# The attention layer's input normalised on GpSimd from pair 8 on, between pieces of GpSimd's preparation work

## The chip, the cores and the metric

The program runs on one core of one Trainium2 chip. The time is the device time of one execution in microseconds. The kernel before took 462.44 us, the median of three runs (461.45 to 463.85).

## The reference

The input x has 32 batches of 256 nodes with 128 features, and there is one 256x256 adjacency matrix. Two layers follow each other, each with a layer norm and a residual:

```
h = max(layernorm(x), 0)
x = x + GAT(h, adj)            # Wh = h W; e = leakyrelu(s1_i + s2_j), masked by adj; softmax(e) Wh
h = max(layernorm(x), 0)
x = x + GCN_LSTM(h, adj)       # twice relu(adj (h Wg + b)), then LSTMs over windows of 1, 2, 3, 4 nodes
```

The layer norm has no weights: (x - mean) / sqrt(var + 1e-5), over the 128 features of a node.

## The kernel before, in words

All of x lies in SBUF in the tensor `xs`, as 64 tiles of 128 nodes by 128 features. Four tiles make a pair of batches, so there are 16 pairs. The attention layer is `phase_a`. Each engine runs its part of it as a software pipeline written out by hand with the helper `ticks`: in tick t an engine works on several stages of different pairs, `live(s)` meaning pair t - s. The engines meet by semaphores alone.

In tick t of `phase_a`, TensorE does in this order: the projection (L926) and the scores' row (L930) of pair t-1, the transposes of the normalised tiles of pair t (L936), the attention's product of pair t-4 (L947) and the transposes of the probabilities of pair t-3 (L959). It waits for `a_v` before the transposes of pair t. VectorE does the two passes over the scores of pair t-1 (L665, L699), with two small operations on 128x4 values between (L673, L677), the reciprocal and the residual of pair t-4 (L706, L713), and the statistics of pair t-5 for the second layer norm (L655). ScalarE copies the projection (L510) and the transposed input (L517, with the ReLU of the layer norm), takes the exponential (L524), normalises pair t (L491, one operation for each of 4 tiles, scale and shift being pointers to one value per partition) and copies the transposed probabilities (L533). `v_norm` holds one pair, so the normalising of pair t waits until pair t-1 is transposed (`a_T`).

GpSimd turns statistics into scale and shift with `norm_scale` (L384 to L393: ten operations on as many columns as there are tiles, one of them a power, L392). For the first layer it does so in groups of 4, 4, 8, 16, 16 and 16 tiles. Then it prepares constants of the second layer in one go: row sums (L407 to L411), the graph weights (L416 to L420), the biases (L422 to L429), the adjacency in the order of the LSTM's windows (L441, L442) and the weights of the first LSTM (L451, L452). Only then comes `norm_scale` for the second layer, for 16 tiles at a time, each time after a wait for the statistics. Then it splits the other LSTM weights. GpSimd issues no DMA. `phase_b`, the graph layer and the first LSTM, follows `phase_a` in the same way and is the first to use all of these constants.

Of the kernel before, what the change touches and what calls it, by code (L numbers as in the profile page):

```python
# [5 lines left out]
def preln_gat_gcn_lstm_kernel(  # L6
# [22 lines left out]
    fp32 = mybir.dt.float32  # L29
    fp32r = mybir.dt.float32r  # L30
    ALU = mybir.AluOpType
# [3 lines left out]
    P = 128  # L35
    assert D == P and N == 2 * P
    TILES = B * N // P
    PAIRS = B // 2
    NODES = B * N
    QUARTER = TILES // 4  # L40
# [10 lines left out]
    GCN_LOADS = 10  # L51
# [7 lines left out]
    with ctx:  # L59
# [7 lines left out]
        xs = sb("xs", [P, TILES, D])  # L67
# [11 lines left out]
        v_norm = sb("v_norm", [P, 4, D])  # L79
# [3 lines left out]
        adjP_hi = sb("adjP_hi", [P, 2, N], fp32r)  # L83
        adjP_lo = sb("adjP_lo", [P, 2, N], fp32r)
        adj_neg = sb("adj_neg", [P, 2, N])
        adjT_hi = sb("adjT_hi", [P, 2, N], fp32r)
        adjT_lo = sb("adjT_lo", [P, 2, N], fp32r)
# [4 lines left out]
        wg_raw = sb("wg_raw", [P, 2, D])  # L92
        wg_hi = sb("wg_hi", [P, 2, D], fp32r)
        wg_lo = sb("wg_lo", [P, 2, D], fp32r)
        b_raw = sb("b_raw", [P, 2, D])
        b_full = sb("b_full", [P, 2, D])
        b_zeros = sb("b_zeros", [P, D])
        b0_parts = sb("b0_parts", [P, D], fp32r)
        b1_parts = sb("b1_parts", [P, 4, D], fp32r)
# [3 lines left out]
        ident = sb("ident", [P, P])  # L103
        ident_r = sb("ident_r", [P, P], fp32r)
# [41 lines left out]
        RUN = [0, 22, 43]  # L146
# [73 lines left out]
        stored = sem("stored")  # L220

        BESIDE = 4

# [131 lines left out]
        @block.gpsimd  # L357
        def _(pool):
            n = 0

            def done(ins):
                nonlocal n
                n += 1
                ins.then_inc(pool_step, 1)
                pool.wait_ge(pool_step, n)

            done(nc.gpsimd.memset(ident[:, :], 0.0))
            nc.gpsimd.affine_select(out=ident[:, :], in_=ident[:, :], compare_op=ALU.not_equal, fill=1.0, base=0,
                                    pattern=[[-1, P]], channel_multiplier=1).then_inc(ident_ok, 1)
            done(nc.gpsimd.memset(b_raw[:, :, :], 0.0))  # L370
            done(nc.gpsimd.memset(b_zeros[:, :], 0.0))
            nc.gpsimd.nop().then_inc(b_zero, 1)
            nc.gpsimd.memset(wh[:, :, :, D + 2:D + 3], 1.0)
            nc.gpsimd.memset(ones[:, :].bitcast(fp32), 1.0).then_inc(ones_ok, 1)
            done(nc.gpsimd.memset(half[:, :], -0.5))


            def norm_scale(which, lo, cnt):
                st = stats[:, which, lo:lo + cnt, :]
                me, qe, mo, qo = st[:, :, 1], st[:, :, 2], st[:, :, 4], st[:, :, 5]  # L380
                a, b, c, d = (v[:, 0:cnt] for v in (ln_a, ln_b, ln_c, ln_d))
                sc, sh = scale[:, which, lo:lo + cnt], shift[:, which, lo:lo + cnt]

                done(nc.gpsimd.tensor_tensor(b, me, mo, ALU.subtract))  # L384
                nc.gpsimd.tensor_tensor(a, qe, qo, ALU.add)
                done(nc.gpsimd.tensor_tensor(d, b, b, ALU.mult))
                nc.gpsimd.tensor_scalar(a, a, 1.0 / D, EPS, ALU.mult, ALU.add)
                done(nc.gpsimd.tensor_scalar(d, d, 0.25, 0.0, ALU.mult, ALU.add))
                nc.gpsimd.tensor_tensor(c, me, mo, ALU.add)
                done(nc.gpsimd.tensor_tensor(a, a, d, ALU.add))  # L390
                nc.gpsimd.tensor_scalar(c, c, -0.5, 0.0, ALU.mult, ALU.add)
                done(nc.gpsimd.tensor_tensor(sc, a, half[:, 0:cnt], ALU.pow))  # L392
                nc.gpsimd.tensor_tensor(sh, c, sc, ALU.mult).then_inc(ln_ok, cnt // 4)  # L393
                pool.wait_ge(ln_ok, which * PAIRS + (lo + cnt) // 4)

            for c, (lo, cnt) in enumerate(X_GROUPS):
                pool.wait_ge(stats_ok, lo + cnt)
                norm_scale(0, lo, cnt)
                if c == FIRST:
                    pool.wait_ge(adjT_in, 16)  # L400
                    done(nc.gpsimd.tensor_copy(adjT_hi[:, :, :], adjT_raw[:, :, :]))
                    nc.gpsimd.tensor_tensor(adjT_lo[:, :, :], adjT_raw[:, :, :], adjT_hi[:, :, :].bitcast(fp32),
                                            ALU.subtract).then_inc(adjT_ok, 1)


            pool.wait_ge(rs_read, 1)
            done(nc.gpsimd.tensor_copy(rs_full[:, :].bitcast(fp32r), rs_raw[:, :]))  # L407
            for b in range(2):
                done(nc.gpsimd.tensor_copy(rs_parts[0:64, b], rs_full[0:64]))
                done(nc.gpsimd.tensor_copy(rs_parts[96:P, b], rs_full[96:P]))  # L410
                done(nc.gpsimd.tensor_tensor(rs_parts[64:96, b], rs_raw[64:96], rs_full[64:96], ALU.subtract))  # L411
            nc.gpsimd.nop().then_inc(rs_ok, 1)


            pool.wait_ge(gcn_w_in, GCN_LOADS * 16)
            done(nc.gpsimd.tensor_copy(wg_hi[:, :, :], wg_raw[:, :, :]))  # L416
            nc.gpsimd.tensor_tensor(wg_lo[:, :, :], wg_raw[:, :, :], wg_hi[:, :, :].bitcast(fp32), ALU.subtract)
            nc.gpsimd.tensor_copy(ident_r[:, :], ident[:, :])
            nc.gpsimd.tensor_tensor(bl[:, :], bl_raw[:, 0], bl_raw[:, 1], ALU.add)
            done(nc.gpsimd.tensor_copy(b_full[:, :, :].bitcast(fp32r), b_raw[:, :, :]))  # L420

            done(nc.gpsimd.tensor_copy(b0_parts[0:32], b_full[0:32, 0]))  # L422
            done(nc.gpsimd.tensor_tensor(b0_parts[32:64], b_raw[32:64, 0], b_full[32:64, 0], ALU.subtract))
            done(nc.gpsimd.tensor_copy(b0_parts[64:P], b_full[64:P, 0]))
            for k in range(4):

                done(nc.gpsimd.tensor_copy(b1_parts[64:P, k], b_zeros[64:P]))
                done(nc.gpsimd.tensor_copy(b1_parts[0:32, k], b_full[0:32, 1]))
                done(nc.gpsimd.tensor_tensor(b1_parts[32:64, k], b_raw[32:64, 1], b_full[32:64, 1], ALU.subtract))  # L429
            nc.gpsimd.nop().then_inc(b_ok, 1)  # L430

            pool.wait_ge(adjT_ok, 1)
            pool.wait_ge(adj_neg_ok, 1)
            for part, placed in ((adjT_hi, adjP_hi), (adjT_lo, adjP_lo)):
                by_t = part[:, :, 0:252].rearrange("p u (a q j) -> p u j q a", q=3, j=4)
                for u in range(2):
                    to = placed[:, u].rearrange("p (j m) -> p j m", j=4)
                    for q in range(3):  # L440
                        nc.gpsimd.tensor_copy(to[:, :, RUN[q]:RUN[q] + 21], by_t[:, u, :, q, :].bitcast(fp32))  # L441
                ins = nc.gpsimd.tensor_copy(placed.rearrange("p u (j m) -> p u j m", j=4)[:, :, :, 21],  # L442
                                            part[:, :, 252:256].bitcast(fp32))
            done(ins)
            nc.gpsimd.nop().then_inc(adjP_ok, 1)

            def split_weights(p, m):
                i, j = (p - 1) // 2, (p - 1) % 2
                for c in range(2):
                    g = slice(c * 2 * D, (c + 1) * 2 * D)  # L450
                    done(nc.gpsimd.tensor_copy(wl_of[0][i][:, j, m, g], wraw[:, m, p - 1, g]))  # L451
                    ins = nc.gpsimd.tensor_tensor(wl_of[1][i][:, j, m, g], wraw[:, m, p - 1, g],  # L452
                                                  wl_of[0][i][:, j, m, g].bitcast(fp32), ALU.subtract)
                ins.then_inc(wl_ok, 1)


            pool.wait_ge(lstm_w_in, 32)
            split_weights(1, 0)
            pool.wait_ge(wl_ok, 1)

            for c in range(4):
                pool.wait_ge(stats_ok, TILES + (c + 1) * QUARTER)
                norm_scale(1, c * QUARTER, QUARTER)


            pool.wait_ge(one_lo, 1)
            for n_, (p, m) in enumerate((p, m) for p in range(2, SKIPS + 1) for m in range(2)):
                split_weights(p, m)
                pool.wait_ge(wl_ok, n_ + 2)

        @block.scalar
        def _(act):
# [23 lines left out]

            def first_norm(t, ph, live):

                if live(0):
                    if isinstance(t, int):  # L500
                        act.wait_ge(ln_ok, t + 1 if t < 7 else PAIRS)
                    after(act, a_T, t, 0)
                    normalise(0, t, range(4), a_v)

# [630 lines left out]
```

## Time and profile before

| | |
|---|---|
| median of three runs | 462.44 us |
| the profiled execution | 464.01 us, span 462.2 us |
| granted TensorE clock, mean of the span | 0.978 |
| PE busy | 433.5 us (94%) |
| VectorE busy | 379.4 us (82%) |
| ScalarE busy | 322.9 us (70%) |
| GpSimd busy | 77.6 us (17%) |

`phase_a` takes about the first 110 us, its full pipeline the stretch from 35 to 95 us. A row of the timeline tells when an instruction or a run of equal ones began, how long it took from its first start to its last end, and in brackets the idle time before it. Starts of the same line in two ticks give the length of a tick.

### The profile page before, as it was taken

To read this page: it belongs to the slowest core of one execution; us is meant where nothing else is said; L and a number is where in the kernel's file an instruction comes from. 1 tells how busy PE (TensorE), PEld (TensorE's weight loads), DVE (VectorE), ACT (ScalarE), POOL (GpSimd) and SP (SyncE) were. 2 spreads that over 40 slices of the span, in tenths; PEclk is the share of its full clock that TensorE was granted. 3 is DMA by queue.
4 is the path that set the end of the run, shared out by engine and by line. 5 is a ranking of instruction groups with operands and counts; after the bars stand their busy time and mean duration, and the time that the engine had idled before them with its cause. 6 is when DMAs were issued, how large, how long until landed. Compare 5 with 4: busy or idle time off the path is not lost.

```text
span 462.2 us, 8017 instructions
## 1 busy us (share of the span) xinstructions
PE 433.5 (94%) x2550; PEld 380.9 (82%) x2550; DVE 379.4 (82%) x976; ACT 322.9 (70%) x632; POOL 77.6 (17%) x182
## 2 busy tenths in 40 slices
PE   6579999979998999999999999999999999999991
PEld 5358888879997999999878888899999988887881
DVE  3799999986779878788777888888788788888895
ACT  3479999966787678887676676767667675564550
POOL 5758841230419100000000000000000000000000
PEclk9689999989999999999999999999999999999998
DMA  8910000000000000000000000000000000002116
GB/s 244 333 41 1 2 2 1 0 0 1 1 3 1 0 0 0 0 0 1 0 0 2 0 2 0 0 1 2 0 1 1 1 1 1 0 23 69 45 48 182
DMA packets 14075, 11.68 MB, mean 25 GB/s; under 512 B 982, under 2 KB 12252, under 8 KB 13788
## 3 DMA queue, kind: packets, MB, share of 16 engines
q1 hardware_dynamic: 11404, 9.97, 7.1%
q10 hardware_dynamic: 2640, 1.33, 1.1%
q8 instruction: 16, 0.26, 0.3%
q14 instruction: 15, 0.12, 0.1%
HBM read 7.10 MB, written 4.19 MB: 24 GB/s over the span
## 4 chain that ended last, share of the span: by engine, by line
PE 69%; DVE 18%; ACT 4%; issue 3%; DMA 3%; DVEq 1%; SPq 1%; ACTq 0%
PE ps L967 47%; PE ps L1089 11%; PE ps L1093 6%; DVE score L699 4%; DVE score L665 3%; DMA xs<-in_x 3%; DVE xs L713 3%; DVE stats L655 2%; PE ps L947 2%; ACT v_norm L491 1%; ACT work L596 1%; DVE xs L848 1%; PE ps L1011 1%; ACT prob L524 1%; PE ps L1007 1%
## 5 line engine op out<-in xcount | busy, mean ns | idle before, releaser
L596 ACT ACTIVATE work<-ps,bl 128x512 f32<-128x512 f32 (+2 forms) x204 | 111.2, 628 | 30.8 <-PE ps L1093 23.4
L967 PE MATMUL ps<-h_hi,wl_hi 128*128 128x512 f32 (+3 forms) x252 | 94.5, 375 | 4.0 <-DVE h_lo L759 3.2
L967 PE MATMUL ps<-h_lo,wl_hi 128*128 128x512 f32 (+3 forms) x252 | 93.9, 372 | 0.0
L967 PE MATMUL ps<-h_hi,wl_lo 128*128 128x512 f32 (+3 forms) x252 | 93.8, 372 | 0.0
L586 ACT ACTIVATE work<-work 128x512 f32<-128x512 f32 (+2 forms) x56 | 31.5, 570 | 44.3 <-DVE work L843 33.6
L967 PEld LDWEIGHTS ps<-h_hi,wl_hi 128*128 128x128 f32 x252 | 47.5, 188 | 11.5 <-issue 3.2
L967 PEld LDWEIGHTS ps<-h_lo,wl_hi 128*128 128x128 f32 x252 | 47.6, 189 | 7.5
L491 ACT ACTIVATE v_norm<-xs,shift,scale 128x128 f32 (+1 forms) x128 | 52.6, 489 | 1.1 <-POOL shift L393 1.0
L967 PEld LDWEIGHTS ps<-h_hi,wl_lo 128*128 128x128 f32 x252 | 47.6, 189 | 6.5
L1089 PE MATMUL ps<-s_hi,wl_hi 128*128 128x512 f32 (+2 forms) x144 | 51.9, 362 | 0.0
L1089 PE MATMUL ps<-s_hi,wl_lo 128*128 128x512 f32 (+2 forms) x144 | 51.4, 359 | 0.0
L569 ACT ACTIVATE s_hi<-ps 128x512 fp32r<-128x512 f32 x48 | 28.4, 601 | 19.9 <-PE ps L967 16.6
L557 ACT ACTIVATE work<-ps,bl 128x512 f32<-128x512 f32 x48 | 30.9, 682 | 9.0 <-DVE work L733 7.6
L947 PE MATMUL ps<-wh,pT 128*128 128x130 f32 x256 | 33.9, 287 | 3.0 <-DVE xs L713 2.5
L947 PEld LDWEIGHTS ps<-wh,pT 128*128 128x128 f32 x256 | 31.1, 196 | 5.7 <-issue 2.9
L1093 PE MATMUL ps<-s_lo,wl_hi 128*128 128x512 f32 (+2 forms) x144 | 34.4, 358 | 0.2 <-DVE s_lo L805 0.2
L794 DVE TENSOR_TENSOR s_hi<-work 128x512 fp32r<-128x512 f32 (+2 forms) x36 | 22.0, 612 | 12.0 <-ACT work L586 11.1
L798 DVE TENSOR_TENSOR work<-work 128x512 f32<-128x512 f32 (+2 forms) x52 | 31.3, 602 | 0.0
L1089 PEld LDWEIGHTS ps<-s_hi,wl_lo 128*128 128x128 f32 x144 | 27.1, 188 | 3.2
L1089 PEld LDWEIGHTS ps<-s_hi,wl_hi 128*128 128x128 f32 x144 | 27.1, 188 | 3.1
L757 DVE TENSOR_TENSOR s_lo<-ps,s_hi 128x512 fp32r<-128x512 f32 x32 | 21.9, 685 | 9.4 <-ACT s_hi L569 9.3
L524 ACT ACTIVATE prob<-score,ebias 128x256 f32<-128x256 f32 x64 | 27.4, 512 | 2.3 <-DVE ebias L677 2.3
(131 smaller groups left out, 968.7 us busy)
## 6 DMA issues: line engine op xcount, KB each, us to landing
result<-xs SPq DMA_DIRECT2D x12, 256.0 KB, 2.3
work<-in_w_ih_t SPq DMA_DIRECT2D x1, 1024.0 KB, 10.0
work<-in_w_hh_t SPq DMA_DIRECT2D x1, 1024.0 KB, 8.7
xs<-in_x SPq DMA_DIRECT2D x2, 256.0 KB, 3.7
xs<-in_x SPq DMA_DIRECT2D x1, 512.0 KB, 7.0
result<-xs SPq DMA_DIRECT2D x4, 128.0 KB, 3.4
result<-xs ACTq DMA_DIRECT2D x4, 128.0 KB, 3.7
adj_raw<-in_adj ACTq DMA_DIRECT2D x1, 256.0 KB, 7.5
```

What stands on the lines that cost most here:

```text
L491: ins = nc.scalar.activation(v_norm[:, k, :], xs[:, bass.ds(i, 1), :].rearrange("p o f -> p (o f)"), ACT.Relu, scale=scale[:, which, bass. ...
L524: ins = nc.scalar.activation(prob[:, m, k], score[:, m, k], ACT.Exp, scale=1.0 - SLOPE, bias=ebias[:, m, k:k + 1])
L557: nc.scalar.activation(one_row(g), ps[:, 4 + g, :], ACT.Tanh if g == G else ACT.Sigmoid, bias=bl[:, g:g + 1]).then_inc(one_act, 1)
L569: nc.scalar.activation(dst, ps[:, s - 1, :], ACT.Copy if s in (1, 3) else ACT.Relu).then_inc(b_hi[s], 1)
L586: nc.scalar.activation(lw[:, par, R_TC, 0:cols], lw[:, par, R_C, 0:cols], ACT.Tanh).then_inc(c_act[par], 1)
L596: nc.scalar.activation(lw[:, par, g, 0:cols], ps[:, 4 * par + g, 0:cols], ACT.Tanh if g == G else ACT.Sigmoid, bias=bl[:, (p - 1) * GATES ...
L794: nc.vector.tensor_tensor(hi, shaped(lw[:, par, O, :]), shaped(lw[:, par, R_TC, :]), ALU.mult).then_inc(c_hi[par], 1)
L798: nc.vector.tensor_tensor(row(r, par, R_H), row(r, par, O), row(r, par, R_TC), ALU.mult).then_inc(c_h[par], 1)
L947: ins = nc.tensor.matmul(psA[:, b, ui * (D + 2):(ui + 1) * (D + 2)], pT[:, 2 * b + uj, ui * P:(ui + 1) * P], wh[:, (ph - 4) % 4, 2 * b + u ...
L967: ins = nc.tensor.matmul(dst, a, b, start=start and n_ == 0, stop=stop and n_ == 2)
L1089: nc.tensor.matmul(ps[:, 4 * par + g, 0:cols], part, s_hi[:, par, 0:cols], start=False, stop=False)
L1093: nc.tensor.matmul(ps[:, 4 * par + g, 0:cols], weights(p, 1, g)[0], s_lo[:, par, 0:cols], start=False, stop=True).then_inc(c_gate[par], 1)
```

## The change

ScalarE normalises only pairs 0 to 7. Pairs 8 to 15 are normalised on GpSimd, by four `tensor_scalar` operations (multiply by scale, add shift) of 128x128 each. They leave out the ReLU, which L517 applies again after the transposes in either kernel. GpSimd's preparation is cut into four pieces, unchanged in their operations, and placed between them. `norm_scale` of the second layer works on 8 tiles at a time: four of its eight calls lie between the pieces, the others behind pair 15.

```diff
-            (the preparation in one go: wg_hi ... b_ok, adjP_ok, split_weights(1, 0))
-            for c in range(4):
-                pool.wait_ge(stats_ok, TILES + (c + 1) * QUARTER)
-                norm_scale(1, c * QUARTER, QUARTER)
+            def first_norm(t):
+                pool.wait_ge(a_T, t)
+                for k in range(4):
+                    i = t * 4 + k
+                    ins = nc.gpsimd.tensor_scalar(v_norm[:, k, :], xs[:, i, :], scale[:, 0, i:i + 1],
+                                                  shift[:, 0, i:i + 1], ALU.mult, ALU.add)
+                ins.then_inc(a_v, 1)
+            def second_scale(h):
+                pool.wait_ge(stats_ok, TILES + 8 * (h + 1))
+                norm_scale(1, 8 * h, 8)
+            first_norm(8)
+            graph_weights()        # L416 to L420
+            second_scale(0)
+            first_norm(9)
+            graph_biases()         # L422 to L429
+            first_norm(10)
+            second_scale(1)
+            first_norm(11)
+            adjacency_order()      # L441, L442
+            first_norm(12)
+            second_scale(2)
+            first_norm(13)
+            step_weights()         # L451, L452 for the first LSTM
+            first_norm(14)
+            second_scale(3)
+            first_norm(15)
+            for h in range(4, 8):
+                second_scale(h)
 (ScalarE)
-                if live(0):
-                    if isinstance(t, int):
-                        act.wait_ge(ln_ok, t + 1 if t < 7 else PAIRS)
+                if live(0) and isinstance(t, int) and t < ON_POOL:      # ON_POOL = 8
+                    act.wait_ge(ln_ok, t + 1)
                     after(act, a_T, t, 0)
                     normalise(0, t, range(4), a_v)
```

## Rows read from the trace of the kernel before

**Rows 1.** Windows; us, then busy time (and instructions) of each engine, TensorE's clock, DMA
```profile
70.00:80.00 10.00, 10.00 (x79) 8.75 (x77) 10.00 (x48) 10.00 (x24) 0.70 (x4) 1.00 0.00 1
```

**Rows 2.** Timeline of VectorE; start us, us, instruction, idle before
```profile
44.60 0.44 DVE L673 SCALAR_TENSOR_TENSOR low<-m,wh 128x4 f32<-128x4 f32 x1
...
60.07 0.15 DVE L673 SCALAR_TENSOR_TENSOR low<-m,wh 128x4 f32<-128x4 f32 x1
...
68.52 0.17 DVE L706 RECIPROCAL rinv<-ps 128x4 f32<-128x4 f32 x1
...
70.01 0.15 DVE L673 SCALAR_TENSOR_TENSOR low<-m,wh 128x4 f32<-128x4 f32 x1
...
94.92 0.17 DVE L673 SCALAR_TENSOR_TENSOR low<-m,wh 128x4 f32<-128x4 f32 x1
```

**Rows 3.** Timeline of ScalarE, one tick
```profile
64.86 0.59 ACT L510 ACTIVATE wh<-ps 128x520 f32<-128x520 f32 x1
...
67.46 1.64 ACT L491 ACTIVATE v_norm<-xs,shift,scale 128x128 f32 x4
69.00 1.01 ACT L533 ACTIVATE pT<-ps 128x1024 f32<-128x1024 f32 x1
69.91 0.59 ACT L510 ACTIVATE wh<-ps 128x520 f32<-128x520 f32 x1
```

**Rows 4.** Timeline of TensorE, the transposes of pairs 7, 9, 10 and 11
```profile
49.47 0.60 PE L936 MATMUL ps<-ident,v_norm 128*128 128x128 f32 x4
...
59.69 0.60 PE L936 MATMUL ps<-ident,v_norm 128*128 128x128 f32 x4
...
64.73 0.60 PE L936 MATMUL ps<-ident,v_norm 128*128 128x128 f32 x4
65.18 2.06 PE L947 MATMUL ps<-wh,pT 128*128 128x130 f32 x16
...
68.84 1.02 PE L930 MATMUL ps<-hT,wa 128*128 128x512 f32 x2
69.70 0.60 PE L936 MATMUL ps<-ident,v_norm 128*128 128x128 f32 x4
```

**Rows 5.** Timeline of GpSimd; starts of the pieces, and one call for 8 tiles
```profile
11.57 0.21 POOL L384 TENSOR_TENSOR ln_b<-stats 128x8 f32<-128x8 f32 x1
...
13.49 1.64 POOL L392 TENSOR_TENSOR scale<-ln_a,half 128x8 f32<-128x8 f32 x1
15.28 0.21 POOL L393 TENSOR_TENSOR shift<-ln_c,scale 128x8 f32<-128x8 f32 x1
...
43.81 0.40 POOL L416 CAST wg_hi<-wg_raw 128x256 fp32r<-128x256 f32 x1 [0.17 <-POOL rs_parts L411]
...
45.84 0.28 POOL L422 CAST b_parts<-b_full 32x128 fp32r<-32x128 f32 x1
...
52.22 1.69 POOL L441 CAST adjP_hi<-adjT_hi 128x84 fp32r<-128x84 f32 x6 [0.23 <-POOL b_parts L429]
...
55.96 0.40 POOL L451 CAST wl_hi<-work 128x256 fp32r<-128x256 f32 x1 [0.17 <-POOL adjP_lo L442]
...
57.58 0.73 POOL L452 TENSOR_TENSOR wl_lo<-work,wl_hi 128x256 fp32r<-128x256 f32 x1
```

**Rows 6.** Groups of GpSimd by shape; busy us, mean ns
```profile
L429 POOL TENSOR_TENSOR b_parts<-b_raw,b_full 32x128 fp32r<-32x128 f32 x4 | 1.8, 460 | 0.3
...
L418 POOL CAST ident_r<-ident 128x128 fp32r<-128x128 f32 x1 | 0.3, 289 | 0.0
```

**Rows 7.** Timeline, a VectorE operation inside a power of GpSimd
```profile
101.90 0.16 DVE L677 SCALAR_TENSOR_TENSOR ebias<-m,low 128x4 f32<-128x4 f32 x1
...
101.82 2.91 POOL L392 TENSOR_TENSOR scale<-ln_a,half 128x16 f32<-128x16 f32 x1
```

**Rows 8.** Timeline of TensorE behind the gap at 98 us, and the graph layer's first product
```profile
100.12 3.31 PE L947 MATMUL ps<-wh,pT 128*128 128x130 f32 x16 [2.11 <-DVE xs L713]
...
104.43 0.36 PE L967 MATMUL ps<-adjT_hi,s_hi 128*128 128x256 f32 x1
```

More of the change, by code:

```diff
@@ L222, in preln_gat_gcn_lstm_kernel @@
         BESIDE = 4
+        ON_POOL = 8
         def ticks(eng, depth, unroll, body, first=0, beside=None, lag=0):
@@ L412, in _ @@
             nc.gpsimd.nop().then_inc(rs_ok, 1)
[L415 to L445, printed above, removed]
             def split_weights(p, m):
@@ L454, in split_weights, with graph_weights @@
                 ins.then_inc(wl_ok, 1)
-            pool.wait_ge(lstm_w_in, 32)
-            split_weights(1, 0)
-            pool.wait_ge(wl_ok, 1)
-            for c in range(4):
-                pool.wait_ge(stats_ok, TILES + (c + 1) * QUARTER)
-                norm_scale(1, c * QUARTER, QUARTER)
+            def graph_weights():
+                pool.wait_ge(gcn_w_in, GCN_LOADS * 16)
+                done(nc.gpsimd.tensor_copy(wg_hi[:, :, :], wg_raw[:, :, :]))
+                nc.gpsimd.tensor_tensor(wg_lo[:, :, :], wg_raw[:, :, :], wg_hi[:, :, :].bitcast(fp32), ALU.subtract)
+                nc.gpsimd.tensor_copy(ident_r[:, :], ident[:, :])
+                nc.gpsimd.tensor_tensor(bl[:, :], bl_raw[:, 0], bl_raw[:, 1], ALU.add)
+                done(nc.gpsimd.tensor_copy(b_full[:, :, :].bitcast(fp32r), b_raw[:, :, :]))
@@ new lines, in graph_biases @@
+            def graph_biases():
+                done(nc.gpsimd.tensor_copy(b0_parts[0:32], b_full[0:32, 0]))
+                done(nc.gpsimd.tensor_tensor(b0_parts[32:64], b_raw[32:64, 0], b_full[32:64, 0], ALU.subtract))
+                done(nc.gpsimd.tensor_copy(b0_parts[64:P], b_full[64:P, 0]))
+                for k in range(4):
+                    done(nc.gpsimd.tensor_copy(b1_parts[64:P, k], b_zeros[64:P]))
+                    done(nc.gpsimd.tensor_copy(b1_parts[0:32, k], b_full[0:32, 1]))
+                    done(nc.gpsimd.tensor_tensor(b1_parts[32:64, k], b_raw[32:64, 1], b_full[32:64, 1], ALU.subtract))
+                nc.gpsimd.nop().then_inc(b_ok, 1)
@@ new lines, in adjacency_order @@
+            def adjacency_order():
+                pool.wait_ge(adjT_ok, 1)
+                pool.wait_ge(adj_neg_ok, 1)
+                for part, placed in ((adjT_hi, adjP_hi), (adjT_lo, adjP_lo)):
+                    by_t = part[:, :, 0:252].rearrange("p u (a q j) -> p u j q a", q=3, j=4)
+                    for u in range(2):
+                        to = placed[:, u].rearrange("p (j m) -> p j m", j=4)
+                        for q in range(3):
+                            nc.gpsimd.tensor_copy(to[:, :, RUN[q]:RUN[q] + 21], by_t[:, u, :, q, :].bitcast(fp32))
+                    ins = nc.gpsimd.tensor_copy(placed.rearrange("p u (j m) -> p u j m", j=4)[:, :, :, 21],
+                                                part[:, :, 252:256].bitcast(fp32))
+                done(ins)
+                nc.gpsimd.nop().then_inc(adjP_ok, 1)
@@ new lines, in step_weights @@
+            def step_weights():
+                pool.wait_ge(lstm_w_in, 32)
+                split_weights(1, 0)
+                pool.wait_ge(wl_ok, 1)
+            def first_norm(t):
+                pool.wait_ge(a_T, t)
+                for k in range(4):
+                    i = t * 4 + k
+                    ins = nc.gpsimd.tensor_scalar(v_norm[:, k, :], xs[:, i, :], scale[:, 0, i:i + 1],
+                                                  shift[:, 0, i:i + 1], ALU.mult, ALU.add)
+                ins.then_inc(a_v, 1)
```

## The prediction

> **What bounds the kernel now.** The change touches only the attention layer, so the first view to read is the busy time by stretches, from 70 to 80 us, where its pipeline is full [rows 1]. There TensorE, VectorE and ScalarE all show 10.00 of 10 us. A share of 100% doesn't say who sets the pace, since the ends of pipelined instructions overlap, so the second view is the timeline of each engine, read for the length of a tick.
>
> VectorE starts its small L673 at 60.07 and at 70.01 us, two ticks apart: 4.97 us a tick, with nothing idle in its rows; from there to 94.92 us five ticks take 24.91 us, 4.98 each [rows 2]. ScalarE goes from L510 at 64.86 to L510 at 69.91 us, 5.05 us, also with nothing idle [rows 3]. TensorE goes from transposes at 64.73 to transposes at 69.70 us, 4.97 us [rows 4]. So VectorE has work for 4.97 us a tick, ScalarE for a little more, and it alone has something taken from it: L491, 1.64 us for four tiles, of which about 1.54 us count, since L533 starts at 69.00, 1.54 us behind L491's start at 67.46 [rows 3].
>
> **What the change takes away.** Eight ticks lose 1.54 us on ScalarE, 12.3 us of its work. That gives back only what ScalarE costs over VectorE. From 60.07 to 94.92 us seven ticks took 34.85 us; at 4.97 us they would take 34.79 [rows 2]. The gain there is 0.1 us: with ScalarE out of the way VectorE bounds the tick at the same length. This is what I expect of the removed work.
>
> There is a second small gain. L673 of 44.60 us took 0.44 us instead of 0.15 [rows 2], beside a GpSimd operation of the preparation that started at 43.81 us [rows 5]; in the changed kernel GpSimd stands still there, because the first piece now waits for the transposes of pair 7. That is 0.29 us back. Together 0.4 us.
>
> **What it adds on GpSimd, and when it must be ready.** GpSimd now works to a deadline: the transposes of pair t on TensorE wait for it, and behind them in TensorE's order stand the attention's product, the probabilities' transposes, the next projection and the next scores, thus what VectorE and ScalarE wait for. The pieces' prices come from [rows 5], start to start: graph weights 43.81 to 45.84, 2.05 us; biases 45.84 to 52.22, less the wait ahead of the last, 6.25 us; adjacency 52.22 to 55.96, 3.75 us; first LSTM weights 55.96 to 57.58 + 0.73, 2.4 us; scale and shift of 8 tiles 11.57 to 15.28 + 0.21 and 0.08 for the last signal, 4.0 us.
>
> The new operation, a `tensor_scalar` of 128x128 with pointers, is nowhere in the trace. The cheap bound is a cast of 128x128, one tensor in and one out, 289 ns, or about 0.25 us start to start, 1.0 us for four. The dear bound is an operation with two tensor inputs of 128 columns, 460 ns, about 0.42 us start to start, 1.7 us for four [rows 6]. I take 1.2 us: it reads one tensor like the cast, and two pointers on top. The Trainium skill (GPSIMD Engine Reference, 3.1, the side-by-side cycle accounting) puts a body of up to two operations at 1.03 cycles per element and a two-input one at about 2.6; by that it would stay at the cheap end, and the sum would be 1.2 us smaller than mine. It says nothing of pointers.
>
> Now the schedule, in the times of the profile before. Pair 7 is transposed by 49.47 + 0.60 = 50.07 us [rows 4]. GpSimd starts pair 8 at 50.15 and ends at 51.35; graph weights until 53.4; scale 0 until 57.4; pair 9 until 58.6, in time for its transposes at 59.69 [rows 4]. Then the biases until 64.95, and pair 10 until 66.15. TensorE wanted it at 64.73 [rows 4] and gets it at 66.25: **1.5 us late**. This is the worst place, since the 6.25 us piece alone is longer than a tick.
>
> From there GpSimd has between two pairs a piece plus 1.2 us plus 0.1 for the signal, against a tick of 4.97:
> - pair 11 behind scale 1: 5.3, another 0.25 to 0.33 late, I take 0.25
> - pair 12 behind the adjacency: 5.05, another 0.1
> - pair 13 behind scale 2: 5.3, another 0.33
> - pair 14 behind the LSTM weights: 3.7, 1.3 us to spare
> - pair 15 behind scale 3: 5.3, covered by what was spared.
>
> In sum TensorE is 2.2 us late at the end. How much of it reaches VectorE? The attention's product has slack: started at 65.18 it ends by 67.24, and L706 reads it at 68.52 [rows 2, 4], so 1.3 us of 1.5 are hidden there. But the next scores have next to none: L930 ends at 68.84 + 1.02 = 69.86, and L673, which waits for it, starts at 70.01 [rows 2, 4]. So 0.1 us is hidden and 2.1 us arrive. Nothing gives them back: a tick of VectorE is full at 4.97 us, and the graph layer begins when the pipeline has drained.
>
> **Contention.** Each tick VectorE runs L673 and L677, small but with both inputs in SBUF. Beside the preparation one took 0.44 instead of 0.15 us [rows 2]. GpSimd is now busy through ticks 9 to 15. At up to 0.29 us a tick this is 0 to 2 us; I take 0.3, since in the late ticks VectorE waits for TensorE anyway and only the last three or four count. The Trainium skill (SBUF — State Buffer, Who interferes with whom) says that a VectorE instruction with two SBUF inputs contends with a GpSimd instruction that reads SBUF, and that the loser is blocked for the whole of the other. The 0.44 us agrees. Held to the letter it would hold for the power as well, four of them, now placed in full ticks. The trace disagrees: L677 of 101.90 us took 0.16 us in the middle of a power of 2.91 us that started at 101.82 [rows 7].
>
> **The second layer's scale and shift.** Eight calls at 4.0 us are 32 us of GpSimd. Four of them are in the schedule above; the other four, 16 us, lie behind pair 15 in time in which GpSimd has nothing else, and each can start as soon as its statistics are there. I cost these at nothing; without that cover they would be 16 us. The constants moved back (biases by 65, adjacency by 75, first weights by 84 us) are all ready before the first product of the graph layer at 104.43 us [rows 8]; that costs nothing, and 20 us later it would still cost nothing.
>
> **The sum.** -0.4 + 2.1 + 0.3 = +2.0 us. The profiled execution took 464.01 us (span 462.2), 1.6 us over the median of the runs, and no term depends on that; from the median I forecast 462.44 + 2.0 = **464.4 us**.
>
> **Rivals.**
> - *Dear operations on GpSimd.* At 1.7 us for four, pair 10 is 3.0 us late, pairs 11, 12 and 13 another 0.75, 0.6 and 0.83, pair 15 another 0.2: 5.4, less 0.1 hidden, less 0.4, with 0.3 of contention: +5.2 us, 467.6. For it speaks that the pointers' cost is unknown; against it that they aren't tensors. Every 0.1 us in the four operations is worth 0.6 us here.
> - *Nothing is late* (not slower). If the pieces run in less, or the early ticks run late themselves, so that pair 10 comes in time, only the 0.4 us of gain is left, and perhaps 0.2 us more in ticks 8 and 9: 461.8. It decides from pair 10: the chain of 16.1 us from 50.15 to 66.25 must fit into 14.6 us. Even at 1.0 us for four it is 15.5, so this needs shorter pieces as well. Against it stands that they are measured.
> - *The clock drops.* Behind the gap of 2.11 us at 98 us, the product L947 took 3.31 instead of 2.06 us [rows 4, 8]. If the gap of 1.5 us ahead of pair 10 does that too, 1.3 us for the product and some 0.6 behind it come on top: +3.9 us, 466.3. The gap is shorter than the one that did it, and that is all there is against it.
> - *The power blocks VectorE.* This is what the page on SBUF makes of it: powers of 8 tiles beside L673 or L677. Up to 1.64 us each [rows 5] in four ticks; at half of that, and where they meet two times in three, +2 us on top, 466.4. The row above speaks against it.
>
> **Chances.** Forecast, +1 to +3 us: 0.48. Dear operations: 0.20. Nothing late, or faster than that: 0.19. Clock: 0.09. Power: 0.04. A change is told from none at about 0.5%, 2.3 us here. Slower by more: dear operations, clock and power (0.33) and a bit under a quarter of the forecast (0.10), 0.43. Faster by more needs something that the profile doesn't show; 0.08. The rest, 0.49, is within. The range, from the case in which nothing is late to the dear one: 461.7 to 467.4.
>
> **What would show it.** Right: transposes L936 of pair 10 that wait 1 to 2 us for GpSimd, L673 of VectorE idle 1 to 1.5 us behind L930 in the next tick, ScalarE with about 1.5 us idle in each tick from 8 on, ticks of 4.97 us on VectorE where GpSimd is in time. Four operations of pair 8 that take together 1.2 us, and the phase's end about 2 us later. Wrong: no wait of TensorE for GpSimd, VectorE ticks under 4.9 us, or an end of the phase that didn't move; or a tick that is longer with no TensorE wait in it, which would be contention.

## The result and the profile after

The changed kernel took 468.31 us (median of 4 runs, 467.15 to 469.05) against 462.35 us; the ratio is 1.0115, 95% interval 1.009 to 1.014. Timed again beside the experiments it took 467.04 us against 462.79, ratio 1.0086 (1.0064 to 1.0107). So the change costs 4.0 to 5.3 us by the ratios; the medians themselves lie 4.25 and 5.96 us apart. I had forecast +2.0 us, 464.4, in a range up to 467.4: slower it is, and by twice that or more. The rival of dear operations gave 467.6.

The first view of after is the timeline of TensorE, the transposes of pairs 7 to 15, which answers to [rows 4]. A start less the one above it is the tick; brackets give what it waited for.

```profile
48.92 0.60 PE L968 MATMUL ps<-ident,v_norm 128*128 128x128 f32 x4
53.93 0.60 PE L968 MATMUL ps<-ident,v_norm 128*128 128x128 f32 x4
59.20 0.66 PE L968 MATMUL ps<-ident,v_norm 128*128 128x128 f32 x4 [0.25 <-POOL v_norm L470]
67.17 0.66 PE L968 MATMUL ps<-ident,v_norm 128*128 128x128 f32 x4 [2.89 <-POOL v_norm L470]
72.88 0.66 PE L968 MATMUL ps<-ident,v_norm 128*128 128x128 f32 x4 [0.64 <-POOL v_norm L470]
78.34 0.65 PE L968 MATMUL ps<-ident,v_norm 128*128 128x128 f32 x4 [0.39 <-POOL v_norm L470]
84.06 0.66 PE L968 MATMUL ps<-ident,v_norm 128*128 128x128 f32 x4 [0.64 <-POOL v_norm L470]
88.97 0.60 PE L968 MATMUL ps<-ident,v_norm 128*128 128x128 f32 x4
93.92 0.65 PE L968 MATMUL ps<-ident,v_norm 128*128 128x128 f32 x4
```

Over the 4.97 us of a full tick the ticks are longer by 0.04, 0.30, 3.00, 0.74, 0.49, 0.75, -0.06 and -0.02 us, 5.24 in sum. The same nine rows of before span 49.47 to 89.70 us, 0.47 over eight full ticks. The phase thus lost 4.77 us, in ticks in which TensorE waits for GpSimd. The two profiled spans differ by less, 465.3 against 462.2 us: pair 7 began 0.55 us earlier, and TensorE's clock gave back 1.2 us behind the phase (experiments 10 to 12).

Why GpSimd comes late is in its own timeline, around pair 10:

```profile
57.40 1.75 POOL L470 TENSOR_SCALAR v_norm<-xs,scale,shift 128x128 f32<-128x128 f32 x4
59.09 0.28 POOL L434 CAST b_parts<-b_full 32x128 fp32r<-32x128 f32 x1
...
64.72 0.44 POOL L441 TENSOR_TENSOR b_parts<-b_raw,b_full 32x128 fp32r<-32x128 f32 x1
65.38 1.73 POOL L470 TENSOR_SCALAR v_norm<-xs,scale,shift 128x128 f32<-128x128 f32 x4 [0.21 <-POOL b_parts L441]
67.08 0.21 POOL L385 TENSOR_TENSOR ln_b<-stats 128x8 f32<-128x8 f32 x1
```

and one operation's price in the groups by shape (busy us, mean ns):

```profile
L470 POOL TENSOR_SCALAR v_norm<-xs,scale,shift 128x128 f32<-128x128 f32 x32 | 14.0, 450 | 7.2 <-PE ps L968 6.2 <-POOL b_parts L441 0.2 <-POOL adjP_lo L454 0.2
```

Four operations hold GpSimd for 1.69 us (57.40 to 59.09); I had taken 1.2. The pieces have the prices of [rows 5]: the biases 59.09 to 65.38, 6.29 us with the wait ahead of the last, against 6.38 there.

Windows of after, which answer to [rows 1], show that the three engines which were all full no longer are, ScalarE by intent, the other two by waiting:

```profile
70.00:80.00 10.00, 8.97 (x68) 7.32 (x67) 8.36 (x41) 6.30 (x13) 9.13 (x31) 1.00 0.00 1
80.00:90.00 10.00, 9.36 (x74) 8.01 (x73) 9.13 (x40) 6.84 (x14) 9.07 (x23) 1.00 0.00 1
```

The fifth column, GpSimd, is now the full one: 9.1 of 10 us. VectorE's timeline, which answers to [rows 2], has the wait where the prediction put it: L738, the reciprocal, waits 1.48 us for the attention's product, and L705 0.98 us for the scores.

```profile
69.65 0.18 DVE L738 RECIPROCAL rinv<-ps 128x4 f32<-128x4 f32 x1 [1.48 <-PE ps L979]
72.28 0.17 DVE L705 SCALAR_TENSOR_TENSOR low<-m,wh 128x4 f32<-128x4 f32 x1 [0.98 <-PE ps L962]
```

### The profile page after: what moved, and what is told of

It reads as the page before. It is cut to its first block, busy times and chain, and to the rows that moved or that the text cites. A ratio compares the mean times of both kernels' runs of the same rounds, so it can differ in the third digit from the quotient of the medians.

```text
span 465.3 us, 8002 instructions
## 1 busy us (share of the span) xinstructions
PE 429.8 (92%) x2550; PEld 376.8 (81%) x2550; DVE 380.3 (82%) x976; ACT 311.8 (67%) x600; POOL 98.3 (21%) x254
## 4 chain that ended last, share of the span: by engine, by line
PE 73%; DVE 9%; POOL 7%; ACT 4%; DMA 3%; issue 3%; SPq 1%; DVEq 0%; ACTq 0%; POOLq 0%
PE ps L999 47%; PE ps L1121 11%; PE ps L1125 5%; PE ps L979 3%; DMA xs<-in_x 3%; POOL v_norm L470 2%; PE ps L962 1%; ACT work L628 1%; DVE score L731 1%; PE ps L991 1%; DVE score L697 1%; POOL scale L393 1%; DVE xs L880 1%; ACT v_norm L524 1%; PE ps L958 1%
## 5 line engine op out<-in xcount | busy, mean ns | idle before, releaser
L524 ACT ACTIVATE v_norm<-xs,shift,scale 128x128 f32<-128x128 f32 (+1 forms) x96 | 39.4, 487 | 1.2 <-POOL shift L394 1.1
L979 PE MATMUL ps<-wh,pT 128*128 128x130 f32 x256 | 32.1, 278 | 3.1 <-DVE xs L745 2.5
L979 PEld LDWEIGHTS ps<-wh,pT 128*128 128x128 f32 x256 | 29.9, 190 | 5.0 <-ACT pT L565 2.9
```

The costliest lines, as they stand in the source:

```text
L524: ins = nc.scalar.activation(v_norm[:, k, :], xs[:, bass.ds(i, 1), :].rearrange("p o f -> p (o f)"), ACT.Relu, scale=scale[:, which, bass. ...
L979: ins = nc.tensor.matmul(psA[:, b, ui * (D + 2):(ui + 1) * (D + 2)], pT[:, 2 * b + uj, ui * P:(ui + 1) * P], wh[:, (ph - 4) % 4, 2 * b + u ...
```

## The experiments

In all comparisons the kernel before ran on the same chip.

**1. Weights and biases ahead of pair 8** (early_prep).

```diff
+            graph_weights()
+            graph_biases()
             first_norm(8)
-            graph_weights()
             second_scale(0)
             first_norm(9)
-            graph_biases()
             first_norm(10)
```

> Graph weights and biases are put ahead of pair 8, into the 6 us in which GpSimd otherwise waits for the transposes of pair 7; nothing else is changed, all eight pairs stay on GpSimd and all of its work stays. Theory (the loss is lateness of GpSimd against TensorE's order): the chain ahead of pair 10 loses 6.25 us and every pair comes in time, so the transposes of pairs 10 to 15 wait for nothing, ticks are 4.97 to 5.02 us, and the time is 462.2 us, within 0.6 of the kernel before. Rival (a GpSimd that is busy in each tick slows VectorE through shared access to SBUF, or a normalised tile from GpSimd is late whatever the order): the ticks 9 to 15 stay 0.3 us or more longer and the time stays at 464.5 us or above.

Measured: 463.66 us against 462.92, ratio 1.0015 (1.0002 to 1.0027). The theory had asked for 462.2 us and for no more than 0.6 over before, and it is 0.74. But most of the loss is gone with two pieces moved, so lateness was most of the cause. No tick waits for GpSimd by more than 0.17 us. But one tick, from 69.70 to 75.99 us, is 1.3 us too long without a wait of TensorE for GpSimd. VectorE's timeline and then GpSimd's at the same place:

```profile
70.02 1.55 DVE L705 SCALAR_TENSOR_TENSOR low<-m,wh 128x4 f32<-128x4 f32 x1
```

```profile
69.75 0.20 POOL L454 CAST adjP_hi<-adjT_hi 128x8 fp32r<-128x8 f32 x1
69.88 1.67 POOL L453 CAST adjP_lo<-adjT_lo 128x84 fp32r<-128x84 f32 x6
71.48 0.20 POOL L454 CAST adjP_lo<-adjT_lo 128x8 fp32r<-128x8 f32 x1
```

An operation on 128x4 values, 0.15 us elsewhere, lasts 1.55 us, to 71.57 us: until the second six of the fourteen copies end (71.55), which GpSimd issues with no wait between them. That is contention, as the rival had it, but in one block and not in every tick; the next experiments take it up. For the busy GpSimd as such the rival had asked for 0.3 us more in every tick, which isn't there.

**2. Only the second part** (act_norms_all): the new order and the calls for 8 tiles, ScalarE normalising all pairs.

```diff
-            first_norm(8)   # ... and the seven others on GpSimd
-                if live(0) and isinstance(t, int) and t < ON_POOL:
-                    act.wait_ge(ln_ok, t + 1)
+                if live(0):
+                    if isinstance(t, int):
+                        act.wait_ge(ln_ok, t + 1 if t < 7 else PAIRS)
```

> Only the second part of the change: the pieces in their new order and eight calls for 8 tiles, but ScalarE normalises all 16 pairs as in the kernel before. Theory (lateness of the normalised pairs is the whole loss): 462.4 us, the same as before, since nothing of GpSimd is then awaited in the ticks. Rival (the eight calls or the interleaved preparation cost by themselves, through contention or a late scale of the second layer): 463.5 us or more, with a wait for GpSimd or longer ticks in the trace.

Measured: 462.84 us against 462.92, ratio 1.0003 (0.999 to 1.0016). The new order and the halved calls cost nothing. The pieces don't fall in quite the same ticks, since GpSimd has no pairs to wait for here: the adjacency's copies run from 62.38 us, in the change from 72.77. The transposes of pairs 7 and 15 start at 48.63 and 88.85 us, 40.22 us apart, as before (40.23).

**3. Constants for the pointers** (const_scale).

```diff
-                    ins = nc.gpsimd.tensor_scalar(v_norm[:, k, :], xs[:, i, :], scale[:, 0, i:i + 1],
-                                                  shift[:, 0, i:i + 1], ALU.mult, ALU.add)
+                    ins = nc.gpsimd.tensor_scalar(v_norm[:, k, :], xs[:, i, :], 1.0,
+                                                  0.0, ALU.mult, ALU.add)
```

> The changed kernel with the constants 1.0 and 0.0 in the place of the two pointers in the four operations of a pair on GpSimd; the layer norm of pairs 8 to 15 is thereby left out. It asks why four operations take 1.68 us start to start and not 1.2. If the pointers are dear: 289 to 310 ns for one, 1.1 us for four, and with 0.55 us less in each pair the lateness falls from 5 to about 2 us, time 464.5 us. If the operation is as dear with constants: 430 ns, time 468.2 us, same as the change.

Measured: 463.15 us against 462.92, ratio 1.0009 (0.9994 to 1.0023). The groups by shape, and the one wait that is left, of pair 10:

```profile
L470 POOL TENSOR_SCALAR v_norm<-xs 128x128 f32<-128x128 f32 x32 | 8.7, 300 | 7.2 <-PE ps L968 6.4 <-POOL b_parts L441 0.2 <-POOL adjP_lo L454 0.2
```

```profile
65.28 0.66 PE L968 MATMUL ps<-ident,v_norm 128*128 128x128 f32 x4 [1.25 <-POOL v_norm L470]
```

The pointers are the price: 300 ns with constants, close to the cast of [rows 6], and 450 ns with two pointers. The theory holds, but the time is 1.4 us lower than I expected. The transposes of pairs 7 and 15 start at 49.03 and 90.31 us, 41.28 us apart: 3.72 less than in the change, and my figure of 464.5 lay 3.7 under 468.2. Most of the 1.4 us is that start: timed again, the change is at 467.04. The phase still takes 1.05 us more than before and the time only 0.23; TensorE's clock, below, gave 1.2 us back behind the phase, as in the change.

**4. Three calls moved behind pair 15** (scales_last).

```diff
             first_norm(10)
-            second_scale(1)
             first_norm(11)
@@
             first_norm(12)
-            second_scale(2)
             first_norm(13)
@@
             first_norm(14)
-            second_scale(3)
             first_norm(15)
-            for h in range(4, 8):
+            for h in range(1, 8):
```

> The changed kernel with three calls for the second layer's scale and shift (those between pairs 10 and 11, 12 and 13, 14 and 15) moved behind pair 15. Theory (lateness adds up pair by pair): pair 10 is still 2.9 to 3.0 us late, but pairs 11, 12 and 13 no longer (0.74, 0.49, 0.75 us in the trace of the change), so 2.0 us come back: 466.3 us. Rival (only the first large gap counts, the later waits being hidden behind VectorE): no difference to the change, 468.2 us.

Measured: 466.99 us against 462.92, ratio 1.0092 (1.0069 to 1.0114). That lies between the two figures I had set, and is no gain on the change: 467.04 us when that was timed beside the next group. In the trace the lateness did fall: pairs 7 to 15 take 43.58 us (48.95 to 92.53) instead of 45.00, 1.42 of the 2.0 us expected. Here too the two views disagree by what the clock did.

**5. Adjacency behind pair 15 as well** (early_adj_last).

```diff
 (on top of early_prep)
             first_norm(11)
-            adjacency_order()
             first_norm(12)
@@
             first_norm(15)
+            adjacency_order()
```

> Weights and biases ahead of pair 8, as in the run before, and the adjacency's fourteen copies moved behind pair 15. In the run before one L705 of VectorE (128x4, both inputs in SBUF) took 1.55 instead of 0.15 us, from 70.02 us until the end of the seven copies that GpSimd issued back to back. If this block is what was left of the loss: 1.4 us less than early_prep in the same profile, no L705 or L709 over 0.5 us, time 462.3 us, about that of before. If the block only stood where VectorE would have waited anyway: no less than early_prep, 463.7 us.

Measured: 463.26 us against 462.79, ratio 1.0008 (0.9996 to 1.002), where I had 462.3. The block went from its old tick: 40.21 us between the transposes of pairs 7 and 15, against 41.75 in early_prep. But it came back in the next place in which L705 met the copies, and took 1.1 us there. My "none over 0.5 us" was a miss. That the time is still near that of before owes something to the clock, which didn't fall behind the phase here (experiments 10 to 12). VectorE's timeline, then GpSimd's:

```profile
89.01 1.29 DVE L705 SCALAR_TENSOR_TENSOR low<-m,wh 128x4 f32<-128x4 f32 x1
```

```profile
88.61 1.67 POOL L453 CAST adjP_lo<-adjT_lo 128x84 fp32r<-128x84 f32 x6
90.20 0.21 POOL L454 CAST adjP_lo<-adjT_lo 128x8 fp32r<-128x8 f32 x1
```

**6. A wait behind each copy** (early_adj_waits).

```diff
 (on top of early_prep)
-                            nc.gpsimd.tensor_copy(to[:, :, RUN[q]:RUN[q] + 21], by_t[:, u, :, q, :].bitcast(fp32))
+                            done(nc.gpsimd.tensor_copy(to[:, :, RUN[q]:RUN[q] + 21], by_t[:, u, :, q, :].bitcast(fp32)))
```

> The same order as early_prep, with a wait for its own end behind each of GpSimd's adjacency copies. If VectorE is held by the run of copies as one, because the next starts before it gets its turn, it now gets in between two of them: longest L705 or L709 under 0.5 us, GpSimd's piece longer by about 1 us (14 waits of 0.07), no pair late by it, time 462.6 us. If it waits by chance of a single long operation, nothing changes, 463.7 us.

Measured: 463.34 us against 462.79, ratio 1.0006 (0.999 to 1.0022). The longest of VectorE's small operations in the midst of the same copies, L709, in the timeline of VectorE, then the copies in that of GpSimd:

```profile
69.63 0.26 DVE L709 SCALAR_TENSOR_TENSOR ebias<-m,low 128x4 f32<-128x4 f32 x1
```

```profile
69.53 2.29 POOL L453 CAST adjP_lo<-adjT_lo 128x84 fp32r<-128x84 f32 x6
```

With waits between the copies VectorE gets in after 0.1 us. So the block of 1.3 to 1.4 us comes from the run of copies, not from one of them. But the piece grew by 1.2 us (six copies from 1.67 to 2.29 us, twice), which made the pairs behind it late again: TensorE waits 0.7 us for GpSimd, and 41.11 us pass between the transposes of pairs 7 and 15. "No pair late" was wrong, and most of the gain was given back.

**7. ScalarE relieved, GpSimd unchanged** (act_one_tile).

```diff
 (the kernel before)
-                    normalise(0, t, range(4), a_v)
+                    normalise(0, t, range(4 if isinstance(t, int) and t < 8 else 1), a_v)
```

> The kernel before, with ScalarE normalising only one tile of four from pair 8 on (the layer norm of the other three is left out); GpSimd does what it did. It measures what relief of ScalarE alone is worth: 8 x 1.15 = 9.2 us of its work gone. My term for it was 0.1 us: 462.8 us beside 462.9. If ScalarE did set the pace: 2 us or more faster, 460.9 or less.

Measured: 462.44 us against 462.79, ratio 0.9988 (0.9971 to 1.0004). Six ticks from pair 9 to pair 15 take 29.88 us (59.82 to 89.70) against 30.01 in both profiles of before: 0.13 us, for 1.15 us less of ScalarE's work in each tick. The work taken from ScalarE was hardly on the path, as forecast.

**8. The change again** (after_again).

> The changed kernel once more, on the same chip as the other experiments, to have its time beside theirs. Lateness seen in its profile (3.0 us at pair 10, 0.74, 0.49, 0.75 behind) less the 0.1 us that VectorE has to spare, less 0.4 of gain and with up to 0.4 of contention: 5 us over before, 467.9 us. If the first measurement was high by chance: 466.5 us or less, nearer to the 3.1 us that the two profiled spans differ by.

Measured: 467.04 us (466.85 to 467.42) against 462.79, ratio 1.0086 (1.0064 to 1.0107). It lies between the two figures I had set. 45.19 us between the transposes of pairs 7 and 15.

**9. All in time** (all_in_time), with the adjacency's copies awaited, the high and the low parts apart.

(The diff is shortened: the waits behind the copies are left out, and pairs 13 to 15 are a loop in the kernel.)

```diff
+            graph_weights()
+            graph_biases()
             first_norm(8)
-            graph_weights()
-            second_scale(0)
             first_norm(9)
-            graph_biases()
+            adjacency_order([(adjT_hi, adjP_hi)])
             first_norm(10)
-            second_scale(1)
+            adjacency_order([(adjT_lo, adjP_lo)])
             first_norm(11)
-            adjacency_order()
+            step_weights()
             first_norm(12)
-            second_scale(2)
+            second_scale(0)
             first_norm(13)
-            step_weights()
             first_norm(14)
-            second_scale(3)
             first_norm(15)
-            for h in range(4, 8):
+            for h in range(1, 8):
                 second_scale(h)
```

> All eight pairs on GpSimd and all of its work kept, in an order in which by the measured prices nothing is late: weights and biases ahead of pair 8; the adjacency's copies in two halves, each copy awaited, behind pairs 9 and 10; first LSTM weights behind 11; scale and shift for 8 tiles once behind 12 and seven times behind 15. If lateness and the block by back-to-back copies are the whole loss: transposes of pairs 8 to 15 wait for nothing over 0.2 us, no L705 or L709 over 0.5 us, transposes of pair 7 to those of pair 15 40.0 to 40.4 us (40.23 before), time 462.7 us, same as before within 0.15%. If GpSimd's mere activity costs more: 463.5 us or above, and over 41 us between these transposes.

Measured: 462.30 us (12 runs) against 463.08, ratio 0.999 (0.9974 to 1.0005). The transposes in TensorE's timeline, first and last three of pairs 7 to 15:

```profile
49.23 0.60 PE L966 MATMUL ps<-ident,v_norm 128*128 128x128 f32 x4
54.34 0.60 PE L966 MATMUL ps<-ident,v_norm 128*128 128x128 f32 x4
59.24 0.60 PE L966 MATMUL ps<-ident,v_norm 128*128 128x128 f32 x4
...
79.11 0.60 PE L966 MATMUL ps<-ident,v_norm 128*128 128x128 f32 x4
84.08 0.60 PE L966 MATMUL ps<-ident,v_norm 128*128 128x128 f32 x4
89.06 0.60 PE L966 MATMUL ps<-ident,v_norm 128*128 128x128 f32 x4
```

39.83 us, a little under what I gave and 0.4 less than before. No transposes wait for GpSimd, and from 50 us on the longest of the small operations takes 0.30 us. All of the change's work is still on GpSimd, three more of the calls behind pair 15; it is busy for 32.5 of the 45 us from 50 to 95 us, against 40.3 in the change and 38.2 in early_prep, whose other ticks were not 0.3 us longer either. The clock falls behind the phase here as in before, so the comparison is even. With that, lateness is the change's loss in the phase, and the block by runs of copies is what early_prep had left over. The version is as good as the kernel before and not measurably better.

**10 to 12. The clock once more** (scales_last_2, before_2, after_3, unchanged kernels).

> A second look at scales_last, for the clock: in its first profile the product behind the 2.1 us gap at 101 to 103 us took 3.32 us at 0.5 of the clock, in both profiles of the change 2.03 us at full clock behind a gap of the same length. If the drop goes with the order of the work (each kernel has it always or never): 3.3 us again. If it goes by execution: either. Span between the transposes of pairs 7 and 15 43.5 us as before.

> A second look at the kernel before, for the clock: with the drop behind the gap at 98 us (3.31 us for the product) if it goes with the order of the work; either way if it goes by execution. 462.8 us.

> A third look at the change, for the clock: no drop (2.03 us) if it goes with the order of the work. 467.5 us.

Measured: 467.05, 462.69 and 467.71 us, one run each. The product L947, L976 or L979 behind the gap of 2.1 us in the drain of the phase, in the timeline of TensorE of before_2, scales_last_2 and after_3:

```profile
99.91 2.50 PE L947 MATMUL ps<-wh,pT 128*128 128x130 f32 x16 [2.10 <-DVE xs L713]
```

```profile
103.19 3.29 PE L976 MATMUL ps<-wh,pT 128*128 128x130 f32 x16 [2.06 <-DVE xs L742]
```

```profile
105.97 2.03 PE L979 MATMUL ps<-wh,pT 128*128 128x130 f32 x16 [2.06 <-DVE xs L745]
```

The gap is the same in all, but the granted clock falls from 2.4 to 1.2 GHz behind it in two of two profiles of before and two of two of scales_last, and in none of three of the change. In before_2 it fell later into the product, which took 2.50 us and not the 3.31 that I gave. The other traces have the same gap, 2.06 to 2.11 us: the clock falls behind it in act_norms_all, act_one_tile, early_prep, early_adj_waits and all_in_time, and not in const_scale and early_adj_last, one profile each. So it goes with the order of the work, as far as kernels were profiled more than once, and not simply with whether GpSimd normalises.

Its price, by VectorE's casts of the second layer's input, in before and then in the change:

```profile
100.64 0.43 DVE L767 CAST s_hi<-v_norm 128x512 fp32r<-128x512 f32 x1 [0.66 <-ACT v_norm L491]
108.30 0.43 DVE L767 CAST s_hi<-v_norm 128x512 fp32r<-128x512 f32 x1 [0.84 <-ACT v_norm L491]
113.47 0.43 DVE L767 CAST s_hi<-v_norm 128x512 fp32r<-128x512 f32 x1 [0.84 <-ACT v_norm L491]
```

```profile
104.95 0.43 DVE L799 CAST s_hi<-v_norm 128x512 fp32r<-128x512 f32 x1 [0.71 <-ACT v_norm L524]
111.11 0.43 DVE L799 CAST s_hi<-v_norm 128x512 fp32r<-128x512 f32 x1 [0.84 <-ACT v_norm L524]
116.61 0.45 DVE L799 CAST s_hi<-v_norm 128x512 fp32r<-128x512 f32 x1 [0.84 <-ACT v_norm L524]
```

From the first to the second, 7.66 us in before and 7.64 in before_2, but 6.16 us in after and 6.17 in after_3. That is 1.5 us back, of which the next step loses 0.3 again: 5.17 us from the second to the third in before, 5.50 in after. So the change gets 1.2 us back there. In all nine profiles in which the clock falls the first step takes 7.60 to 7.67 us, in all five in which it doesn't 6.16 or 6.17. That is why scales_last, 1.4 us ahead of the change at the end of the phase, isn't ahead at the end.

A second thing shows in after_3, alone of the three profiles of the change: the clock also fell behind the 2.97 us wait of pair 10. First windows of TensorE (busy, clock), then VectorE's timeline:

```profile
67.00:68.00 1.00, 0.74 (x7) 1.00 0.00 0
68.00:69.00 1.00, 1.00 (x9) 0.65 0.07 16
69.00:70.00 1.00, 1.00 (x6) 0.50 0.00 0
70.00:71.00 1.00, 1.00 (x7) 0.50 0.00 0
71.00:72.00 1.00, 1.00 (x8) 0.64 0.00 0
```

```profile
74.03 0.56 DVE L705 SCALAR_TENSOR_TENSOR low<-m,wh 128x4 f32<-128x4 f32 x1 [1.45 <-PE ps L962]
...
74.85 1.46 DVE L709 SCALAR_TENSOR_TENSOR ebias<-m,low 128x4 f32<-128x4 f32 x1
```

The product behind it took 3.15 instead of 1.96 us. That moved VectorE's small operations into the adjacency's copies (72.89 to 76.44 us), which they miss in the first profile of the change (72.28 and 77.99 us), and L709 took 1.46 us instead of 0.15. In this execution 46.62 us pass between the transposes of pairs 7 and 15 (48.88 to 95.50), 1.6 more than in the first. scales_last_2 had the drop behind pair 10 too, and 44.46 us between these transposes where I had given 43.5. That makes two of five profiles of kernels with that wait. It may be part of the difference between executions of the change at 467 and at 469 us, but that isn't shown: after_3, with the drop and the block, took 467.71 us, and no slower execution was profiled. Other stretches vary too: from the second of VectorE's casts to the sixteenth before took 102.42 us and before_2 101.36.

## Why the prediction was wrong

- **The step that failed** is the price of the new operation: "I take 1.2 us" for four, near the cast. Measured 1.69 us, 450 ns each, at the dear bound of [rows 6]. Everything that hangs on it was mis-sized alike: with 1.7 us the same working gives 3.0, 0.75, 0.6 and 0.83 us of lateness for pairs 10 to 13, and 3.00, 0.74, 0.49 and 0.75 were measured. Only pair 15 came in time where the rival gave 0.2; its own terms, 0.83 us more against 0.77 to spare, give less than 0.1. The sum lacked the 1.2 us that the clock gave back, so part of the closeness of its 467.6 to the 467.04 and 468.31 measured is luck.
- **The reason for the choice was wrong.** I reasoned that pointers aren't tensors. Experiment 3 shows that the two pointers make the whole difference, 150 ns for each operation. The rule of the Trainium skill (GPSIMD Engine Reference, 3.1), 1.03 cycles per element for a body of up to two operations, had put the operation at the cheap end. With constants it lies there, 300 ns beside the cast's 289; with two pointers, 450 ns, it doesn't.
- **The mechanism was right:** the first gap ahead of pair 10, behind the biases; TensorE's order carrying it on; VectorE with 0.1 us to spare at the scores; pair 14 recovering.
- **The gain from ScalarE** was sized right: 0.1 us forecast, 0.13 in experiment 7. The second small gain, 0.29 us, can't be told: in the change no small operation is slow before 59 us, but pair 7 starts at 49.47 us in one profile of before and at 48.90 in the other. Its row was also read beside the wrong operation. The one of 43.81 us had ended at 44.21; L673 stood beside the next, in GpSimd's timeline of before, and both end at 45.0 us:

```profile
44.29 0.73 POOL L417 TENSOR_TENSOR wg_lo<-wg_raw,wg_hi 128x256 fp32r<-128x256 f32 x1
```

- **The second layer's calls at nothing** was right (experiment 2).
- **Contention** was taken as small and even, up to 0.29 us a tick. In the first profile of the change it is (one L709 of 0.44, the rest 0.30 or less). In others it is one block, of 0.6 us in scales_last and of 1.1 to 1.4 us in early_prep, early_adj_last and after_3, which I had no term for. On the power I was right to go by the row: in no profile here does a small operation that starts in the midst of a power take more than 0.24 us. So the rule of the Trainium skill (SBUF — State Buffer, Who interferes with whom), that the loser is blocked for the whole of the other, doesn't hold for it. For the copies it agrees in kind, but there VectorE waited for several of them, and in three profiles for 0.16 us or less in their midst.
- **The clock** I had only as a loss behind pair 10. It does fall there in some executions: the phase then took 46.62 us instead of 45.00 and 45.19, where I had priced 1.9 us. It also gave back 1.2 us in the drain in all three profiles of the change.
- **The biases** stand in the prediction at 6.25 us; [rows 5] give 6.38 with the last wait and 6.15 without. That is worth 0.1 us.
- **Chances:** 0.20 for the rival that came true was too little. A price with bounds of 1.0 and 1.7 us, worth 0.6 us of time for every 0.1, deserved even weight on both ends.

## What to carry to other kernels

Work moved to an idle engine isn't free when others wait for it in order: write down its deadline in each tick, add up its pieces between two deadlines, and put pieces longer than a tick where the engine stands still. Relief of an engine is worth only what that engine costs over the next one; where three engines are full at 4.97 to 5.05 us, taking 1.15 us a tick from one gave 0.1 us in six ticks. When a sum hangs several times on one unmeasured price, give the forecast at both bounds the same care.

## What the runs showed of the hardware

- A GpSimd `tensor_scalar` of 128x128 fp32 takes 300 ns with two constants and 450 ns with two pointers to a value per partition.
- A VectorE operation with two small inputs in SBUF was held up to 1.4 us by a run of six GpSimd copies without waits between them, and 0.1 us with waits. Seven such operations in six profiles ended within 0.05 us of the end of the run (early_prep, early_adj_last, after_3, scales_last, before_2, act_one_tile). Others got in after 0.16 us or less in the midst of the same run: at 54.83 us in before, 64.38 in act_norms_all, 70.82 in const_scale. What decides that stays open.
- The same gap of 2.1 us was followed by a drop of TensorE's clock in nine profiles of seven kernels and in none of five of three others, the change among them. What in the work ahead of it decides stays open.
